# Cutting a blocking first stage into pieces that run under a scan loop (image, Gram and token-turn jobs in tiles 0 to 18)

## Time and profile before

| | |
|---|---|
| median of 3 runs (lowest to highest) | 5504.55 us (5501.18 to 5506.01) |
| the profiled execution | 5506.06 us, span 5504.3 us |
| busy PE, DVE, POOL, ACT | 87%, 92%, 92%, 65% of the span |
| `prologue` | 0 to 270.7 us |
| start of `mambas` until the first scan | 270.7 to 316.6 us |
| the 56 tiles and `finish` | the rest |
| POOL `make_dbx` | 1792 times, mean 2116 ns |
| DVE `scan` (L1012) | 1792 times, mean 2016 ns |
| DMA | 567.00 MB, mean 103 GB/s |

### The profile page before, as it was taken

One profiled execution on the slowest core, in us unless ns is written; L12 is line 12 of the kernel. 1 busy time (PEld: TensorE's weight loads), 2 busy tenths in 40 slices (PEclk: granted clock), 3 DMA queues, 4 the chain that ended last, 5 costly groups with the idle time before them and its releaser, 6 DMA issues. The chain is left out here.

```text
span 5504.3 us, 70129 instructions
## 1 busy us (share of the span) xinstructions
PE 4768.9 (87%) x25566; PEld 3445.4 (63%) x25566; DVE 5058.5 (92%) x3463; ACT 3552.7 (65%) x5626; POOL 5044.1 (92%) x2469
## 2 busy tenths in 40 slices
PE   8878888888888888888888898889999999999987
PEld 7846566666666656566656666666666666666665
DVE  4469999999999999999999999999999999999995
ACT  0057676766676667676776676767676767676762
POOL 0079999999999999999999999999999999999994
PEclk9989998999999999999999999999999999999998
DMA  4222323232323232323142424242424242424242
GB/s 157 103 91 85 103 80 107 76 108 74 111 72 111 72 115 68 118 65 118 65 128 81 131 82 131 82 137 90 133 91 132 94 131 93 132 93 135 89 135 100
DMA packets 223005, 567.00 MB, mean 103 GB/s; under 512 B 28258, under 2 KB 94690, under 8 KB 221508
## 3 DMA queue, kind: packets, MB, share of 16 engines
q1 hardware_dynamic: 210996, 532.78, 29.7%
q10 hardware_dynamic: 11664, 29.74, 1.4%
HBM read 501.08 MB, written 61.36 MB: 102 GB/s over the span
## 5 line engine op out<-in xcount | busy, mean ns | idle before, releaser
L1066 POOL TENSOR_TENSOR dbx<-dtx,b_all 128x896 f32<-128x896 f32 x1792 | 3719.8, 2116 | 74.9 <-DMA b_all<-bc_scratch 71.6
L1012 DVE TENSOR_TENSOR_SCAN mamba_ps<-mamba_ps,dbx 128x896 f32<-128x896 f32 x1232 | 2483.6, 2016 | 50.1 <-POOL dbx L1066 41.3
L802 PE MATMUL mamba_ps<-ident,hc 128*112 128x128 f32 x14336 | 1887.6, 285 | 558.8 <-POOL hc L1073 545.8
L802 PEld LDWEIGHTS mamba_ps<-ident,hc 128*112 128x112 f32 x14336 | 1675.9, 139 | 850.8 <-POOL hc L1073 606.5
L857 ACT ACTIVATE mamba_ps<-dt,a_next 128x448 f32<-128x448 f32 x1792 | 1069.0, 629 | 633.4 <-DVE hc L1019 517.2
L857 ACT ACTIVATE mamba_ps<-dt,w 128x448 f32<-128x448 f32 x1792 | 1067.4, 629 | 635.3 <-DVE hc L1019 510.0
L1019 DVE TENSOR_TENSOR hc<-mamba_ps,c_all 128x896 f32<-128x896 f32 x1232 | 1342.3, 1090 | 144.7 <-DVE mamba_ps L1012 3.9
L1073 POOL TENSOR_TENSOR hc<-hc,c_all 128x896 f32<-128x896 f32 x560 | 1183.5, 2114 | 0.0
L1012 DVE TENSOR_TENSOR_SCAN hc<-mamba_ps,dbx 128x896 f32<-128x896 f32 x560 | 1123.7, 2015 | 42.8 <-ACT mamba_ps L857 39.9
L697 PE MATMUL mamba_ps<-u,w 128*128 128x448 f32 x1792 | 805.8, 592 | 18.6 <-DMA u<-u_scratch 15.3
L708 PE MATMUL mamba_ps<-x,taps 128*128 128x448 f32 (+3 forms) x1792 | 683.6, 529 | 1.0 <-ACT sz L880 0.5
(11 more groups left out here) (111 smaller groups left out, 2978.7 us busy)
## 6 DMA issues: line engine op xcount, KB each, us to landing
b_all<-bc_scratch SPq DMA_DIRECT2D x448, 448.0 KB, 5.3
c_all<-bc_scratch SPq DMA_DIRECT2D x448, 448.0 KB, 6.4
u<-u_scratch SPq DMA_DIRECT2D x56, 448.0 KB, 3.3
y_scratch<-ytok SPq DMA_DIRECT2D x56, 448.0 KB, 3.3
src<-y_scratch SPq DMA_DIRECT2D x47, 448.0 KB, 5.3
u_scratch<-ub ACTq DMA_DIRECT2D x28, 448.0 KB, 4.7
src<-in_x SPq DMA_DIRECT2D x27, 448.0 KB, 6.7
xb<-in_x ACTq DMA_DIRECT2D x3, 3136.0 KB, 11.8
```

The costliest lines, as they stand in the source:

```text
L802: ins = nc.tensor.matmul(y_ps[j % 2][:, c * 128:(c + 1) * 128], hc[n % HC_RING][:, e * T + c * TCH:e * T + (c + 1) * TCH], ident[:, :], st ...
L1012: nc.vector.tensor_tensor_scan(dst, h, dbx[n % BX_RING][:, :], 0.0, ALU.mult, ALU.add).then_inc(scan_done, 1)
L1066: nc.gpsimd.tensor_tensor(view(dbx[n % BX_RING], 0, [[T, 2], [1, T]]), view(dtx, j * T, [[0, 2], [1, T]]), view(b_all, 2 * g * T, [[T, 2], ...
```

## The change

Images 2 and 3 leave the prologue altogether, and the second half of image 1 too. What is left there: `first_half(0)`, `first_half(1)`, `second_half(0)` and K of image 1. The weight turns of the second Mamba block now ride on pairs of image 1. Groups of positions are 128 wide, not 112, so an image has 12 pairs and one half pair. u of image 0 is written in the image's own order (`u_image`), seven pieces, two banks of four passes each.

The rest are jobs under tiles 0 to 18 (`PLAN`). Each tile has two places, a and b. A job is one of these:

- *gram*: 448 positions of an image are projected (items 0 and 1: a bias product of 512 columns and four products of 256 columns), and added to the sum so far (item 2: five products of 128 columns). ACT takes each item.
- *small*: K is made from the sum, stored and kept.
- *image*: u of 448 positions, two items of two products of 448 columns; ACT adds the bias and stores the piece.

Ten tiles have an image job in place b (3, 4, 7 to 10, 15 to 18), eight have a gram job there (0, 1, 2, 5, 6, 11, 13, 14), and tile 12 has one job. The input of a job (448 KB of x) is loaded by ACT's queue as soon as the job before is through with the buffer.

Since u now lies in image order, each tile of the first Mamba block (tiles 0 to 27) loads its tokens as rows and PE turns them (items t0 and t1, four transposes each; ACT copies them to `u`). SP stores the turned u for the second block. Nothing is changed in tiles 28 to 55.

```diff
 SCHEDULE = {
-    "out1": (17, 20), ..., "dt3": (23, 23), "y1": (25, None), "f0": (26, 26), "f1": (26, 29),
-    "y2": (31, None),
+    "out1": (17, 20), ..., "dt3": (23, 23), "t0": (24, 24), "y1": (25, None), "a0": (25, 26),
+    "f0": (26, 26), "a1": (26, 28), "f1": (26, 29), "a2": (29, 29), "t1": (29, 29), "b0": (30, 30), "b1": (30, 30), "y2": (31, None),
+    "b2": (31, 31),
 }
+PLAN = {
+    0: (("image", 1, 0), ("gram", 2, 0),),
...
+    18: (("image", 3, 5), ("image", 3, 6),),
+}
# prologue, PE
-                first_half(0)
-                first_half(1)
-                second_half(0, 1)
-                first_half(2)
-                second_half(1, 2)
-                first_half(3)
-                second_half(2, 3)
-                second_half(3, None)
+                first_half(0)
+                first_half(1)
+                second_half(0, 1)
# mambas, SP, once a tile
-                    if t + 2 < 2 * TILES:
-                        sp.wait_ge(work_ready, Item(t, "z3").ready())
-                        load_u(t + 2)
+                    if t + 1 < TILES:
+                        save_u(t + 1)
+                    if t + 2 < TILES:
+                        load_tokens(t + 2)
+                    elif t + 2 < 2 * TILES:
                         sp.wait_ge(work_ready, Item(t, "z3").ready())
...
# mambas, PE
+                def turn_tokens(t, k):
+                    if k == 0:
+                        pe.wait_ge(tok_ready, 16 * (t + 1))
+                    b = take(Item(t, f"t{k}"))
+                    for c in range(4):
+                        ins = nc.tensor.matmul(b[:, c * TCH:(c + 1) * TCH], utok[...], ident[0:TCH, 0:TCH], ..., is_transpose=True)
+                def job_item(t, name):
+                    kind, b, i = JOBS[t, name[0]]
+                    k = int(name[1])
+                    if k == 0:
+                        pe.wait_ge(job_in, 16 * (ORDER.index((t, name[0])) + 1))
...
# mambas, ACT: an image item
+                        if k == 0:
+                            upto(act, u_out, 16 * images_before(q))
+                        nc.scalar.activation(res[:, k * T:(k + 1) * T], take(it)[:, 0:T], ACT.Identity, ...)
+                        if k == 1:
+                            load_job(q + 1)
+                            for oc in range(2):
+                                it = Item(t, f"{name[0]}{oc}")
+                                act.wait_ge(work_free[it.slot], it.freed())
+                            act.dma_start(u_img[b]..., res[...]).then_inc(u_out, 16)
# mambas, ACT before the first tile
-                        for name in FRONT:
-                            if name == "xp":
-                                silu_x(t)
-                            take_front(t, name)
+                        for of, name in PRELUDE:
+                            if name in TURN:
+                                if (of, name) == (1, "t0"):
+                                    silu_x(0)
+                                take_tokens(of, int(name[1]))
+                            else:
+                                take_front(of, name)
```

More of the change, by code:

```diff
@@ L69, in fin_of, with has, images_before @@
     return (BATCH - 1, t - PART_FROM, True) if t < FIN_FROM else ((t - FIN_FROM) // TPB, (t - FIN_FROM) % TPB, False)
+HERE = (0,)
+PLAN = {
+    0: (("image", 1, 0), ("gram", 2, 0),),
+    1: (("image", 1, 1), ("gram", 2, 1),),
+    2: (("image", 1, 2), ("gram", 2, 2),),
+    3: (("image", 1, 3), ("image", 1, 4),),
+    4: (("image", 1, 5), ("image", 1, 6),),
+    5: (("gram", 2, 3), ("gram", 2, 4),),
+    6: (("gram", 2, 5), ("gram", 2, 6),),
+    7: (("small", 2, 0), ("image", 2, 0),),
+    8: (("image", 2, 1), ("image", 2, 2),),
+    9: (("image", 2, 3), ("image", 2, 4),),
+    10: (("image", 2, 5), ("image", 2, 6),),
+    11: (("gram", 3, 0), ("gram", 3, 1),),
+    12: (("gram", 3, 2),),
+    13: (("gram", 3, 3), ("gram", 3, 4),),
+    14: (("gram", 3, 5), ("gram", 3, 6),),
+    15: (("small", 3, 0), ("image", 3, 0),),
+    16: (("image", 3, 1), ("image", 3, 2),),
+    17: (("image", 3, 3), ("image", 3, 4),),
+    18: (("image", 3, 5), ("image", 3, 6),),
+}
+JOBS = {(t, place): job for t, jobs in PLAN.items() for place, job in zip("ab", jobs)}
+ORDER = sorted(JOBS)
+ITEMS = {"gram": 3, "small": 3, "image": 2}
+def has(t, name):
+    if name[0] in "ab":
+        return (t, name[0]) in JOBS and int(name[1]) < ITEMS[JOBS[t, name[0]][0]]
+    if name[0] == "t":
+        return t + 2 < TILES
+    return name[0] != "f" or t in FIN_TILES
+def images_before(q):
+    return sum(JOBS[k][0] == "image" for k in ORDER[:q])
 def due(engine, n):
@@ new lines, in second_half @@
+                    pe.wait_ge(k_dve, 3 * b + 3)
+                    for i in range(TPB):
+                        q = TPB * HERE.index(b) + i
+                        for oc in range(2):
+                            upto(pe, ut_taken, 2 * q + oc - 1)
+                            for k in range(2):
+                                last = nc.tensor.matmul(bank(6 + oc)[:, 0:T], kn[b][:, k * CH + oc * 128:k * CH + (oc + 1) * 128],
+                                                        xb[b][:, k * NPOS + i * T:k * NPOS + (i + 1) * T], start=(k == 0), stop=(k == 1))
+                            last.then_inc(ut_ready, 1)
+                        if then is not None and i == 0:
@@ L372, in second_half @@
                             make_r(then)
-                        if then is not None and i == 4:
+                        if then is not None and i == 2:
                             make_k(then)
@@ L458, in take_k @@
[L458 to L461 removed]
+                    nc.vector.tensor_tensor(kn[b][:, 0:2 * CH], bank(4), id2[:, :], ALU.add)
+                    nc.vector.tensor_tensor(kn[b][:, 2 * CH:2 * CH + 2], bank(5)[:, CH:CH + 2], catb, ALU.add)
+                    nc.vector.tensor_tensor(kn[b][:, 2 * CH + 2:2 * CH + 4], bank(5)[:, CH:CH + 2], cstu, ALU.add).then_inc(k_dve, 1)
@@ L473, in first_half @@
                             take_turn(n)
-                        if i == 13 and b in (0, 2):
-                            take_a(b // 2)
+                        if i == PAIRS - 1:
+                            take_a(b)
+                    for _ in steps:
+                        pass
                     dve.wait_ge(mt_step, PAIRS * (b + 1))
@@ L614, in load_src @@
                     b, i, part = fin_of(t)
+                    if t == PART_FROM:
+                        sp.wait_ge(k_saved, 16 * sum(JOBS[k][0] == "small" for k in ORDER))
+                        sp.wait_ge(u_out, 16 * images_before(len(ORDER)))
                     if t > PART_FROM:
@@ new lines, in make_image @@
+                def make_image(t, place, oc, b):
+                    if oc == 0:
+                        if b in (0, 1):
+                            pe.wait_ge(here_in, 16)
+                        else:
+                            made = next(k for k in ORDER if JOBS[k][0] == "small" and JOBS[k][1] == b)
+                            it = Item(made[0], f"{made[1]}2")
+                            pe.wait_ge(work_free[it.slot], it.freed())
+                    bank = take(Item(t, f"{place}{oc}"))
+                    for k in range(2):
+                        ins = nc.tensor.matmul(bank[:, 0:T], now[:, k * CH + oc * 128:k * CH + (oc + 1) * 128], xs[:, k * T:(k + 1) * T],
+                                               start=(k == 0), stop=(k == 1))
+                    ins.then_inc(work_ready, 1)
```

423 lines of the change are left out of this document (262 added, 161 removed), and 2 rows, old and new, of the table SCHEDULE.

## The result

The changed kernel takes **5410.35 us** (median of 4 runs, 5406.67 to 5413.88), the kernel before 5504.68 in the same session: ratio 0.983, 95% interval 0.9817 to 0.9844. The forecast was 5398 with a range of 5360 to 5445. The profiled execution has a span of 5412.1 us, the one before 5504.3: 92.2 less.

What follows compares the result with a forecast made beforehand. Prologue bound by PE, loop by POOL and its b loads, DVE 0.8 us behind. 5504.3 - 147.3 + 4.9 + 36 = 5397.9 for the span, +1.8 outside, runs' median 1.5 lower: 5398 us, range 5360 to 5445.

Steps and rivals of the forecast that it cites:

- The prologue and the start of the loop: First block and start of the tile loop: the prologue gives -147.3 us, the loop's start costs +4.9 us.
- with hardly a gap: Prologue: PE works through it almost without idling, so each us cut there is a us of the end.
- Under the tiles: Tiles with jobs: added work fits, but late job b and its transfers delay DVE and b loads, +36 us.
- The DMA term: Tile ends: transfers ACT issues behind job b push b5 and b6 back, 1.2 us for one, 2.4 for two.
- the two queues share the engines packet by packet: DMA at tile ends: ACT's few packets are not served last and push b5 and b6 back by their full time.
- what would show it: Signs listed for the forecast; among them POOL's b_all waits up from 1.3 to 3 us or more a tile, first 19 tiles.
- two gram items of 2.6 us end at 1504.2, two image items of 1.5 at 1503: Job b on PE, tile 12's clock: from its start at 1499 or 1500; DVE then 2.4 or 1.2 us late.
- the engines' queues are nearly empty at 1495: Tile end, when job b's input is asked for: argument against the rival in which that input takes 6.7 us.
- the chain of job b decides: Rival, tile ends: late input of job b delays y2 and the decays; 5429 to 5462 us, chance 0.19.
- The rival that would have been slower: Tiles with image items: waiting for the previous piece's store makes the scan 8 us late; 5505 to 5530 us, chance 0.03.

Runs made afterwards that it cites:

- e2: Against the changed kernel, the transfers ACT issues behind job b are issued in slot 8 of the next tile; 5406.71 us, ratio 0.9821.
- e9: Against the changed kernel, 4 unused matmuls (6 in tiles 7 and 15) in PE's wait ahead of job b in tiles holding an image job; 5389.34 us, ratio 0.9793.
- e1: Against the changed kernel, the job table is moved so the small job of image 2 is alone in tile 7; 5403.06 us, ratio 0.9818.
- e7: Against the changed kernel, behind a small job the load of job b's input is issued ahead of the store of K; 5408.52 us, ratio 0.9834.
- e8: Against the changed kernel, 9 unused matmuls (12 in tiles 7 and 15) in PE's wait ahead of job b in tiles holding an image job; 5416.54 us, ratio 0.9848.
- e6: Against the changed kernel, y2 stands ahead of job b on PE and job b's copies go to ACT's slot 31; 5424.1 us, ratio 0.9868.
- e4: Against the changed kernel, image 1's pieces go back to the prologue, small jobs are alone, no image + gram pair; 5389.02 us, ratio 0.9791.

## Why the prediction was right

**The prologue and the start of the loop**: -147.3 and +4.9 stood against -149.7 and +5.4. The copies of mt_sb came at 61.49 and 94.17 where 60.7 and 94.8 were forecast, the block's start at 121.06 where it was 123.4. Rows of the same operation, counted out, gave that, with some luck in it. The prediction says that PE works "with hardly a gap", but the profile before has this wait in the first block (PE was also idle for its first 12.82 us):

```profile
36.20 1.12 PE L296 MATMUL pro_ps<-ident,raw_in 128*128 128x128 f32 x4 [5.28 <-DMA raw_a<-in_L_conv_A_log]
```

The changed kernel's profile has the same wait, 8.64 us long (last section). Three profiles with this prologue don't have it, and there the block starts at 110.4 to 110.8, some 12.8 us ahead of the forecast.

**Under the tiles** the term was mis-sized: +36 stood there, 51.9 came. Split by the prediction's own prices (2.4 us for an image in place b, 1.2 for the last one, 2.2 for a gram, a tenth off):

| tiles | forecast, us | measured, us |
|---|---|---|
| 0, 1, 2: image + gram | 5.9 | 12.7 |
| 3, 4, 8, 9, 10, 16, 17, 18: image + image | 16.2 | 14.9 |
| 5, 6, 11, 13, 14: gram + gram | 9.9 | 2.9 |
| 12: gram | 0 | 0.3 |
| 7, 15: small + image | 4.3 | 21.4 |

- The DMA term (22.8 of the image-b tiles and 9.6 of the gram-b tiles, before the tenth) was too large: moving those transfers out of the way gave about 6 us back (e2), so the near agreement of the image + image tiles is partly luck. That the two queues share the engines packet by packet was my reading of the counts in the earlier trace rows, 414 and 352; no run tells it from first come, first served. POOL's wait for b_all rose to 3 and more in four of these eight tiles, as "what would show it" had asked; in tiles 0 to 2, 7 and 15 there was none, since POOL waited for DVE first.
- The step that failed is "two gram items of 2.6 us end at 1504.2, two image items of 1.5 at 1503". It took the duration at the full clock for matmuls that come behind a wait, where the change's tile 1 has 0.50. The start was right: b0 was forecast at 1499, 69.5 us after the dtx mark on tile 12's clock, and came 69.3 after it in tile 1 (the input was asked for 1.2 us sooner than forecast, and took 4.8 us instead of 3.7). The two gram items then took 5.7 and 3.1 us, where the sum had 2.6 each; even at the full clock they take 3.0 (tile 5). Both image items together took 5.0 to 6.1. So DVE was 4.8 us late in tile 1, not 2.4. With the clock held, e9, tiles 0 to 2 cost 4.6 together instead of 12.7; 5.9 had been forecast.
- The profile before had shown the low clock at this place: the eight passes of L802 in the earlier trace rows took 1.96 us behind their gap of 6.72 (0.50 in the window of 1499 to 1501 us), those of the change's tile 7 1.04 (1.00 from 933 us). Its windows of tile 12:

```profile
1494.00:1496.00 2.00, 0.00 (x0) 0.00 (x0) 2.00 (x2) 1.28 (x3) 2.00 (x2) 0.92 0.80 244
1496.00:1498.00 2.00, 0.00 (x0) 0.00 (x0) 1.87 (x2) 0.81 (x2) 2.00 (x2) 0.50 0.02 9
```

  The first of them also answers "the engines' queues are nearly empty at 1495": the DMA engines were busy for 0.80 of the time there, and idle only from 1496.
- Tiles 7 and 15 were treated as any image-b tile and cost 21.4 together. Their input is asked for 7 us later, from issue to the start of job b it takes 7.5 us in tile 7 and 6.0 in tile 15 (in tile 8 4.8), and PE waits 7.4 and 5.9 us. e1 shows that the pair makes it, e7 that the store doesn't; with the clock held 13.6 remain, and the late input is the suspect left for them, not shown: an earlier issue wasn't tried for the small job.
- Gram + gram tiles were forecast at 2.0 each and cost 0.6. Job a there ends so late on PE that the input of b has nearly landed (waits of 0.25 to 0.7 us) and the clock stays up (1.00 in the windows of job b's first item in all five).
- The rival "the chain of job b decides" names the right chain. Its 67 us and more would need it in all 18 tiles; it decided in five, which made 34 of the 52 us.
- The rival that would have been slower (the image items wait for the store of the piece before) didn't show: ACT waited for PE and for DVE, and no row names `u_out`'s store.

The time fell in the range because errors of opposite sign met: 8 us too much in the tiles with two grams or two images, 24 too little in the five others, which leaves 16, and 2 less in the stages ahead of them. That the total came out only 12 us above the forecast is thus luck in part; the transfers, to which it gave most of the loop's cost, made the smaller part.

## What to carry to other kernels

Where work is slid under a loop, list for each new piece what PE waits for ahead of it and what stands behind it in order; a tile with more work and no gap can cost less than one with less work and a gap (here tiles of two grams, with waits of up to 0.7 us, cost 0.6 each, tiles of an image and a gram, with waits of 2.8 to 4.7 us, 4.2 each). A duration read from a busy stretch may not hold behind a wait of PE (here eight passes took 3.2 to 3.4 us at a clock of 1.00 and 6.28 at 0.50): read the granted clock of the stretch, and price the piece at both levels. If a wait can't be removed, a little unused work in it, shorter than the wait, can pay for itself (e9, 21.8 us off the loop), and more of it than fits costs (e8, 10.1 us on it).

## What the runs showed of the hardware that I had not expected

- 4 unused matmuls in the wait of a tile (6 in two tiles) took 22 us off the loop; 9 and 12 of them added 10.
- PE waits of nearly the same length (3.25 and 3.54 us in one run) left the clock at 1.00 once and at 0.50 the other time, and the next eight passes took 3.27 or 6.28 us.
- Identical prologues ended at two times. In the change's profile, and in most others, PE waited for the weights' loads in the first block and went on at the low clock (0.50 from 36 to 40 us in the change); in e1, e6 and e8 it didn't (nor in e4, whose prologue is longer), and the block ended at 110.4 to 110.8 instead of 118.6 to 121.1. The changed kernel's row, which has no counterpart in e1:

```profile
36.14 1.11 PE L339 MATMUL pro_ps<-ident,raw_in 128*128 128x128 f32 x4 [8.64 <-DMA raw_a<-in_L_conv_A_log]
```

  The load of raw_a, 32 KB, took 14.7 us to land there and 8.6 in e1; over all profiles it took 7.0 to 8.6 in the four without the wait and 13.3 to 15.1 in the others, the kernel before among them (14.6). The code up to this point is the same in all changed kernels; why it lands sooner in some executions is open. It can make 8 to 10 us of the spread of whole-run times, and as much may be to be had there; no run tried.
- A transfer of 16 of 448 columns landed only some 1.6 us sooner than the whole one: PE's wait in the image + image tiles went from 4.07 to 5.83 us (mean 4.65) down to 2.66 to 3.54 (mean 3.07).
